# Three edits of order in a four-layer kernel: layer 0's theta and phi earlier in its loop, layer 1's first values between its scores, layer 2's first normalisation at the end of layer 1

## The reference

```python
# layer 0: attention between x and ctx over channels, then a batch norm over all batches
theta = Wtheta @ x + btheta;  phi = Wphi @ ctx + bphi;  g = Wg @ x + bg
y = softmax(phi.T @ theta) @ g.T
w = Wz @ y.T + bz
x = batchnorm(w) + x
# layer 1: latents (x) attend to [ctx, latents], 16 heads; then RMS norm and an MLP 512 -> 2048 -> 512
a = attention(q(latents), k(h), v(h), mask) @ out_w + out_b + latents
x = gelu(rmsnorm(a) @ w1 + b1) @ w2 + b2 + latents
# layer 2: a recurrent block
xa = layernorm(x);  sx = shifted(xa) - xa
t = tanh((xa + sx * maa_x) @ maa_w1)          # five mixes of 32
xm = xa + sx * (maa_stack + t @ maa_w2)       # inputs of k, w, v, r, g
...                                           # decayed sums over tokens, group norm, gate, feed forward
# layer 3: grouped attention on ctx, residual, layer norm
```

## Time and profile before

| | |
|---|---|
| time, median of 3 runs | 2301.31 us (2297.07 to 2303.19) |
| the profiled execution: its time, its span | 2297.31 us, 2295.5 us |
| TensorE, matmuls: busy, share | 2164.2 us, 94% |
| TensorE, weight loads (beside matmuls) | 1575.0 us, 69% |
| VectorE; ScalarE; POOL busy | 1132.5 us, 49%; 1164.1 us, 51%; 567.4 us, 25% |
| mean granted TensorE clock, share of full | 0.971 |
| layer 0; layer 1; layers 2 and 3 | 0 to 194 us; 194 to 1105.6; 1105.6 to 2295.5 |

### The profile page before, as it was taken

One profiled execution on the slowest core, in us unless ns is written; L12 is line 12 of the kernel. 1 busy time (PEld: TensorE's weight loads), 2 busy tenths in 40 slices (PEclk: granted clock), 3 DMA queues, 4 the chain that ended last, 5 costly groups with the idle time before them and its releaser, 6 DMA issues.

```text
span 2295.5 us, 56418 instructions
## 1 busy us (share of the span) xinstructions
PE 2164.2 (94%) x22208; PEld 1575.0 (69%) x22208; DVE 1132.5 (49%) x3132; ACT 1164.1 (51%) x3500; POOL 567.4 (25%) x573
## 2 busy tenths in 40 slices
PE   7886899999999999998579999999999999999986
PEld 3443666677777766776467778777777777777754
DVE  5664334333333333332345566655566655566643
ACT  4553444444444444553223566565566555556644
POOL 0001000011000100100344344443334444334420
PEclk9998899999999999999779999999999999999988
DMA  5531433443333333334401110101110001110100
GB/s 173 175 120 51 119 98 105 106 104 106 93 93 93 93 93 93 94 82 151 134 16 22 22 22 22 26 17 27 22 26 22 23 17 27 22 27 18 21 16 10
DMA packets 188381, 149.11 MB, mean 65 GB/s; under 512 B 85280, under 2 KB 163488, under 8 KB 185888
## 3 DMA queue, kind: packets, MB, share of 16 engines
q1 hardware_dynamic: 177920, 115.49, 19.8%
q10 hardware_dynamic: 8032, 18.35, 2.3%
q0 software_dynamic: 2240, 12.58, 1.6%
HBM read 96.04 MB, written 46.14 MB: 62 GB/s over the span
## 4 chain that ended last, share of the span: by engine, by line
PE 48%; ACT 1%; DVE 1%; issue 1%; POOL 0%; POOLq 0%; DVEq 0%; ACTq 0%
PE bank L1574 13%; PE bank L1580 12%; PE bank L1567 4%; PE quad L1702 4%; PE quad L1707 2%; PE quad L1821 2%; PE bank L1837 1%; PE quad L1698 1%; PE bank L1603 1%; PE quad L1623 1%; PE bank L1725 1%; PE quad L1712 1%; PE bank L1737 1%; PE bank L1642 1%; PE bank L1650 1%
## 5 line engine op out<-in xcount | busy, mean ns | idle before, releaser
L770 PEld LDWEIGHTS bank<-normedT,mlp_w 128*128 128x128 f32 x2048 | 232.6, 193 | 11.0 <-issue 10.0
L770 PE MATMUL bank<-normedT,mlp_w 128*128 128x128 f32 x2048 | 238.5, 278 | 0.8 <-DVE normedT L1020 0.8
L780 PE MATMUL bank<-mlp_w,geluT 128*128 128x512 f32 x512 | 224.7, 592 | 0.0
L2018 ACT ACTIVATE scores<-scores,nmax 128x128 f32<-128x128 f32 x512 | 198.3, 396 | 2.5 <-DVE nmax L2280 2.5
L1506 POOL TENSOR_TENSOR k_even_odd<-k_even_odd,decay_products 128x512 f32<-128x512 f32 x80 | 98.1, 1226 | 327.4 <-PE quad L1702 251.5
L780 PEld LDWEIGHTS bank<-mlp_w,geluT 128*128 128x128 f32 x512 | 95.0, 190 | 108.1 <-issue 108.1
L971 DVE CUSTOM_DVE_ANT_0 probs<-quad,neg_mask 128x256 f32<-128x256 f32 x256 | 90.8, 420 | 109.8 <-PE quad L725 109.8
L886 ACT ACTIVATE probs<-probs,nmax 128x256 f32<-128x256 f32 x256 | 126.6, 496 | 12.2 <-DVE nmax L971 11.8
L1434 POOL TENSOR_TENSOR gn_rstd<-gn_var_eps,halfs 128x32 f32<-128x32 f32 x16 | 87.0, 5435 | 170.1 <-DVE gn_var_eps L2203 170.1
L2168 DVE TENSOR_TENSOR rT<-rT,decay_products 128x256 f32<-128x256 f32 x96 | 40.9, 426 | 176.2 <-PE quad L1702 71.7
L2280 DVE CUSTOM_DVE_ANT_0 scores<-quad,mask 128x128 f32<-128x128 f32 x512 | 111.0, 286 | 31.9 <-PE quad L1821 31.9
(11 more groups left out here) (241 smaller groups left out, 4528.7 us busy)
## 6 DMA issues: line engine op xcount, KB each, us to landing
l_blocks<-probs_turned_blocks SPq DMA_DIRECT2D x128, 256.0 KB, 2.7
probsT<-l_blocks SPq DMA_DIRECT2D x256, 128.0 KB, 3.5
x_in<-in_x SPq DMA_DIRECT2D x32, 256.0 KB, 2.9
mlp_w<-in_mlp_w POOLq DMA_DIRECT2D x8, 1024.0 KB, 5.5
ctx_in<-in_ctx SPq DMA_DIRECT2D x16, 256.0 KB, 2.9
l_out<-wy ACTq DMA_DIRECT2D x16, 256.0 KB, 2.2
hT<-in_ctxT SPq DMA_DIRECT2D x16, 256.0 KB, 3.6
wy_in<-l_out SPq DMA_DIRECT2D x16, 256.0 KB, 4.0
```

The lines of the kernel that those rows point to most:

```text
L770: mm = nc.tensor.matmul(ps[:, f * P:(f + 1) * P], mlp_w1[:, c, m * P:(m + 1) * P], nT[:, c, :], start=(c == 0), stop=(c == NC - 1))
L780: mm = nc.tensor.matmul(PS[u.bank][:, :], gT[:, f, :], mlp_w2[:, f, :], start=(f == 0), stop=(f == NF - 1))
L2018: ac = nc.scalar.activation(s, s, ACT.Exp, bias=nmax[:, k, 2 * c + e:2 * c + e + 1], scale=-1.0, accum_out=rsum[:, kv, gr:gr + 1])
```

## The change

1. Layer 0, TensorE: `theta_phi(i + 1)` stands ahead of `out_y(i - 1)` and `scores(i, (2, 3))` instead of behind them. ScalarE: `copy_g(i)` comes ahead of `copy_y(i - 1)`, with a wait for `out_y` of its own (it overwrites the g that `out_y` reads), and `theta(i + 1)` waits until the second half of the scores has read the old theta.
2. Layer 1, TensorE: `values(0, 1)` between the two halves of batch 0's scores; ScalarE: `copy_latents(1)` before the second four groups of exponentials.
3. The norm of layer 2's batch 0 moves to the end of layer 1, on all engines, with the centring of Wv. The tiles of the norm are now made outside the layers, and four tiles of layer 1 share their memory (`wyin` with x, `xin1` with nx, `lat` with sx, `latb` with z). ScalarE no longer waits for the last store; SyncE does, before it issues the later stages' weights, which moves them from ScalarE's queue to SyncE's. Step 0 of the pipeline is now only `after_first`; waits for its zeros and constants go to the pieces that use them.

```diff
@@ layer0, tensor
                     turn_probs(i - 1, (2, 3))
+                    theta_phi(i + 1)
                     out_y(i - 1)
                     scores(i, (2, 3))
-                    theta_phi(i + 1)
                     g_proj(i + 1)
                     out_z(i - 1)
@@ layer0, scalar
                 def copy_g(i):
+                    if not isinstance(i, int) or i > 0:
+                        act.wait_ge(O.ready, O.written(i - 1, 1))
                     G.begin(i)
...
                     exp(i, 1)
+                    copy_g(i)
                     copy_y(i - 1)
-                    copy_g(i)
                     if not last:
+                        act.wait_ge(F.ready, F.written(i, 4))
                         theta(i + 1)
                         phi(i + 1)
@@ layer1, sync
                 move_probs(B - 1)
+                def load_x2(i):
+                    sp.dma_start(x2[:, :], l1_out[i]).then_inc(s_x, 16)
+                    sp.dma_start(row12[:, :], a["row1"][i]).then_inc(s_x, 16)
+
+                sp.wait_ge(s_lat, B)
+                sp.wait_ge(s_store, 48)
+                load_x2(0)
                 sp.wait_ge(O.free, O.read(B - 1, 2))
                 for t, n in zip((q_w, k_w, v_w, out_w), ("Wk", "Wr", "Wv", "Wg")):
                     sp.dma_start(t[:, :, :], a[n]).then_inc(s_w2, 16)
+                sp.wait_ge(s_nx1, 1)
+                sp.wait_ge(s_first1, 1)
+                load_x2(1)
@@ layer1, gpsimd
                 rms(B - 1)
+                pool.wait_ge(s_var1, 1)
+                nc.gpsimd.tensor_tensor(rstd2[:, :], ve2[:, :], halfs[:, 0:1], ALU.pow).then_inc(s_rstd1, 1)
+                pool.wait_ge(s_x, 32)
+                nc.gpsimd.tensor_copy(xaT2[:, :, 0], row12[:, :]).then_inc(s_first1, 1)
@@ layer1, tensor
                 scores(0, 0)
+                values(0, 1)
                 scores(0, 1)
-                values(0, 1)
                 turn_latents(1)
...
                 for j in range(4):
                     hidden(B - 1, j)
+                pe.wait_ge(s_nx1, 1)
+                pe.wait_ge(SR.free, SR.read(B - 1, NG))
+                for c in range(NC):
+                    mm = nc.tensor.transpose(PS[0][:, c * P:(c + 1) * P], nx2[:, c * P:(c + 1) * P], ident[:, :])
+                mm.then_inc(s_turn2, 1)
                 for j in range(4):
                     mlp_out(B - 1, j)
@@ layer1, scalar
                 copy_v(0, 1)
+                copy_latents(1)
                 for g in range(4, NG):
                     exps(0, g)
-                copy_latents(1)
...
                     gelu(B - 1, j)
+                act.wait_ge(s_turn2, 1)
+                for c in range(NC):
+                    ac = nc.scalar.activation(xaT2[:, c, 1:P + 1], PS[0][:, c * P:(c + 1) * P], ACT.Identity,
+                                              bias=C("ln1_b", c), scale=C("ln1_w", c))
+                ac.then_inc(s_xa2, 1)
                 store(B - 1)
-                act.wait_ge(s_store, 16 * (B + 1))
@@ layer1, vector
+                def first_norm():
+                    dve.wait_ge(s_x, 32)
+                    nc.vector.bn_stats(st62[:, :], x2[:, :]).then_inc(s_dveN, 1)
...
+                    dve.wait_ge(s_rstd1, 1)
+                    nc.vector.tensor_scalar(nx2[:, :], x2[:, :], mv2[:, 0:1], rstd2[:, :], ALU.subtract, ALU.mult).then_inc(s_nx1, 1)
...
+                    dve.wait_ge(s_w2, 16 * 4)
...
+                        nc.vector.tensor_tensor(wv, wv, wvm[:, c, :, :].unsqueeze(2).to_broadcast([P, NC, D2, HC]), ALU.subtract)\
+                            .then_inc(s_wv, 1)
+                    dve.wait_ge(s_latb2n, B)
+                    dve.wait_ge(s_xa2, 1)
+                    dve.wait_ge(s_first1, 1)
+                    nc.vector.tensor_tensor(sx2[:, :, :], xaT2[:, :, 0:P], xaT2[:, :, 1:P + 1], ALU.subtract).then_inc(s_dveN, 1)
...
                 copy_normed(B - 1)
+                first_norm()
                 output(B - 1)
@@ layers23, steps
-            for i in range(last):
+            segments["after_first"]()
+            for i in range(1, last):
                 step(*(i - k if i >= k else None for k in range(last + 1)))
-                if i == 0:
-                    segments["after_first"]()
@@ layers23, sync
-                load_x(0)
...
                 def after_first():
+                    n_lds0(0, None)
...
+                    sp.wait_ge(s_stored1, 16 * (B + 1))
                     for h in range(HC):
+                        sp.dma_start(W["Wo"][D2 * h:D2 * (h + 1), :, :], a["Wo"][h:P:HC, :, :]).then_inc(s_w3, 16)
+                    for n in ("Wfk", "Wfr", "Wfv"):
+                        sp.dma_start(W[n][:, :, :], a[n]).then_inc(s_w3, 16)
+                    for t, n in ((W["Wq3"], "Wq3"), (Wk3, "Wk3"), (Wv3, "Wv3")):
+                        sp.dma_start(t[:, :, :], a[n]).then_inc(s_w4, 16)
                     sp.wait_ge(s_wg, NC)
@@ layers23, scalar
-                for h in range(HC):
-                    act.dma_start(W["Wo"][D2 * h:D2 * (h + 1), :, :], a["Wo"][h:P:HC, :, :]).then_inc(s_w3, 16)
...
                 def after_first():
-                    act.wait_ge(s_zero, 4)
-                    act.wait_ge(s_setup, SETUP)
+                    pass
```

More of the change, by code:

```diff
@@ L459, in layer1 @@
 def layer1(nc, a, PS, sem, C, R, cols_of, ident, halfs, bn_scale, bn_shift, bn, inputs, load_x, load_ctx, loaded, l1_out,
-           weights, early, s_early, s_w2):
+           weights, early, s_early, s_w2, norm, norm_sems):
     stats, mv, bnt, s_bnv = bn
@@ L467, in layer1 @@
     q_w, k_w, v_w, out_w, mlp_w1, mlp_w2 = weights
+    x2, row12, st62, mv2, ve2, rstd2, nx2, xaT2, sx2, z2 = norm
+    s_x, s_var1, s_rstd1, s_nx1, s_first1, s_z, s_wvm, s_wv, s_dveN, s_stored1 = norm_sems
     NK = 2
@@ L1103, in turn, with layers23 @@
         self.n_ready = self.n_free = 0
-def layers23(nc, a, PS, quad, sem, C, R, CS, col_at, ident, hsum, halfs, l1_out, early, s_early, shared, s_w2):
+def layers23(nc, a, PS, quad, sem, C, R, CS, col_at, ident, hsum, halfs, l1_out, early, s_early, shared, s_w2,
+             norm, norm_sems):
+    x, row1, st6, mv, ve, rstd, nx, xaT, sx, z = norm
+    s_x, s_var1, s_rstd1, s_nx1, s_first1, s_z, s_wvm, s_wv, s_dveN, s_stored1 = norm_sems
     NU = 8
@@ L1907, in p_u1 @@
                 def p_u1(i, uses):
+                    if isinstance(i, int) and i == 0:
+                        act.wait_ge(s_zero, 4)
                     u, ps = use(uses, "p_u1")
@@ L1920, in p_k @@
                 def p_k(i, uses):
+                    if isinstance(i, int) and i == 0:
+                        act.wait_ge(s_setup, SETUP)
                     u, ps = use(uses, "p_k")
@@ L2375, in program @@
         s_w2 = sem("layer2_projections_loaded")
+        x = sb("x_in2", [P, D])
+        row1 = sb("state_row1", [P, NC])
+        st6 = sb("ln1_stats", [P, 6])
+        mv = sb("ln1_mean_var", [P, 2])
+        ve = sb("ln1_var_eps", [P, 1])
+        rstd = sb("ln1_rstd", [P, 1])
+        nx = sb("ln1_x", [P, D])
+        xaT = sb("xaT", [P, NC, P + 1])
+        sx = sb("shifted", [P, NC, P])
+        z = sb("z", [P, NC, P])
+        s_x = sem("n_x_loaded")
+        s_var1 = sem("n_ln1_var_ready")
+        s_rstd1 = sem("n_ln1_rstd_ready")
+        s_nx1 = sem("n_ln1_ready")
+        s_first1 = sem("n_first_row1_ready")
+        s_z = sem("n_z_ready")
+        s_wvm = sem("p_value_weight_sums_ready")
+        s_wv = sem("p_value_weights_centred")
+        s_dveN = sem("n_dve_step")
+        s_stored1 = sem("l1_x_stored")
+        norm = (x, row1, st6, mv, ve, rstd, nx, xaT, sx, z)
+        norm_sems = (s_x, s_var1, s_rstd1, s_nx1, s_first1, s_z, s_wvm, s_wv, s_dveN, s_stored1)
         w1_scope = ctx.enter_context(ExitStack())
```

83 lines of the change are left out of this document (35 added, 48 removed).

## The result

| | before | after |
|---|---|---|
| time, median (4 runs each) | 2299.20 us (2297.07 to 2303.19) | 2270.56 us (2267.56 to 2271.81) |
| profiled execution: time, span | 2297.31, 2295.5 us | 2269.75, 2267.9 us |
| TensorE matmuls busy | 2164.2 us, 94% | 2163.0 us, 95% |

The ratio is 0.9872, with an interval of 0.9852 to 0.9891: the kernel is 1.3% faster. TensorE does the same work. In the profiled pair the span is 27.6 us shorter, 26.4 of them TensorE's waiting, where 35.1 were forecast.

What follows compares the result with a forecast made beforehand. The kernel's time was taken as TensorE's work plus its waits, so only edits that remove or add a wait count. -14 - 2.2 - 18.9 = -35.1 us, from a median of 2301.3 to 2266; range 2256 to 2279.

Steps and rivals of the forecast that it cites:

- Part 1: Layer 0's loop: `theta_phi` ahead of `out_y` cuts the turn from 10.93 to 9.92 us, -14 us over 14 turns.
- S+3.0: Layer 0's turn, counted from S, the start of `out_y`: `scores(2, 3)` end and ScalarE's `theta` starts 3.0 us later.
- The inputs: Layer 0: next inputs land at S+7.4, `theta_phi` needs them at S+8.1, cover 0.7 us; longest landing stalls 0.1.
- rival E: Layer 0's input becomes the loop; at a 7 us landing the turn is 13.3 us and the kernel slower, 2314; chance 0.03.
- Rival B: Layer 0 gives only 9 us, since inputs or copies are later: 2271; chance 0.15.
- Part 2: Layer 1's start: values fill TensorE's wait before the second scores and the store-to-move chain shortens, -2.2 us.
- that chain gains once more: Layer 1's start, SyncE: first store to first move took 3.87 us against 2.57 unhindered; most of these 1.3 us goes.
- Part 3: Layer 1 to layer 2: moving the norm gives -17.4 us, the way to the first projection -1.5; -18.9 in all.
- rival D: Block change: VectorE sits in the centring, waiting for Wv, with `output` behind it, so nothing is won there; chance 0.04.
- rival C: Layer 2's start gives only 12 to 15 us, as POOL's reordering or another early step replaces the norm; chance 0.15.
- The clock at layer 2's start: First mixed product to first projection: -2.1 us if TensorE keeps its clock, 0 if it drops; -1.5 taken.
- Rival A: Layer 0: copies of chunks 0 and 1 don't hold TensorE, so it gives 17.6 us: 2263; chance 0.12.

Runs made afterwards that it cites:

- p1_only: The kernel before with the edits of layer 0 alone: 2291.01 us, ratio 0.9955.
- ctx_late: The changed kernel, with layer 0's input loads asked for one product later in the turn, from the fourth turn on: 2278.70 us, one run.
- no2b: The changed kernel, with ScalarE's `copy_latents(1)` put back behind the remaining exponentials: 2267.72 us, one run.
- x_late: The changed kernel, with SyncE asking for layer 2's first x only when VectorE has read the output product, 12 us later: 2271.25 us, one run.
- gate_again: The changed kernel with VectorE's copies of turned chunks 0 and 1 ahead of its fourth normalisation, timed in the changed kernel's second rounds: 2270.80 us, ratio 0.9871.
- after_again: The changed kernel itself, unaltered, run a second time: 2270.78 us, ratio 0.9871.
- storewait: The changed kernel, with ScalarE waiting again at the end of layer 1 for the last store of x: 2271.45 us, one run.
- actq: The changed kernel, with the 14 later weight loads issued by ScalarE at the start of layer 2 again: 2275.22 us, one run.
- gate: The changed kernel, with VectorE's copies of turned chunks 0 and 1 ahead of its fourth normalisation, first timing: 2267.71 us, ratio 0.9857.

## Why the prediction was right, and where it was off

The forecast was 2266, the measured median 2270.6 (2270.8 in the second set), inside the range of 2256 to 2279; faster, as expected at 0.95. The miss is 4.6 us. By the steps of the sum:

- **Part 1, forecast -14, measured -10.3 in the profiled pair (-10.4 by p1_only's ratio).** The mechanism was right, down to the wait that replaces the removed one: L255 for VectorE's copy, 0.27 where 0.25 was worked out, and L268 waiting in no turn of the loop. Two terms were mis-sized. First, the turn is 10.10, not 9.92: ScalarE's `theta` started 0.15 after the end of the scores rather than at it (S+3.15 for S+3.0), TensorE took up each chunk's turning some 0.14 us after VectorE's copy had ended, and `theta_phi` stood at S+8.29 for S+8.1. I had taken an end in the trace for the moment at which the next engine starts; 0.1 us at each of two handoffs, over 14 turns, is 2.5 us. (3.0 + 0.6 + 1.25 is 4.85, not the 4.87 of the sum; that changes nothing here.) Second, the first turn, where `theta_phi` waited 1.28 us for its input. I had worked out the cover of the inputs for a turn in the middle of the loop only. There `theta_phi` comes 5.36 us after `g_proj`; in the first turn, which has no `out_z` and no wait at L255, it would come after 3.96, from 18.64 to 22.60, and the input asked for at 20.23 landed 3.5 us later. 2.5 and 1.3 are the 3.8 missing. In the nine kernels with part 1 that were slow at the start the wait is 0.4 to 0.8 us (p1_only: 0.62, with a landing of 2.9), in the two others 1.28 and 1.34.
- **The inputs.** Issue at S+4.62 against the worked out S+4.52, landings 2.8, 2.9 and 3.5 (minimum, median, maximum), cover 0.7 forecast and 0.5 to 0.6 by ctx_late. In the loop the inputs bound no turn, so rival E is out for this kernel, though its loop is near: with one more product in front of the request it had begun. Rival B can't be called out. Layer 0's 10.3 is nearer its 9 than the forecast's 14, the total of 2270.6 is its 2271, and a part of its mechanism happened: the copies came 0.11 later than worked out, and the inputs were late in the first turn.
- **Part 2, forecast -2.2, measured -0.6 in the pair and -0.6 over the profiles.** The scores came earlier much as forecast (VectorE's second maxima 0.5 us, first store 0.7 where 0.9 was worked out). The step that failed is "that chain gains once more": I added a gain of 1.3 us on one link without following the chain to its end. In the pair the store-to-move distance fell by only 0.52, from 3.87 to 3.35, and from the moves' issue to their use it took more, 0.12 for the first half (7.54 for 7.42) and 0.45 for the second (238.31 - 229.96 = 8.35 for 249.26 - 241.36 = 7.90). In no2b the distance fell by 1.23, to 2.64, and the first half's landing took 1.25 of it back. Both come to 0.6. The statements that the second half of the attention would start 16 us earlier and the first projection of layer 2 35 us earlier were wrong: it was 10.95 and 27.39.
- **Part 3, forecast -18.9, measured -17.0 in the pair, and -19.5 to -19.8 where the clock stayed** (57.17, 57.11 and 56.88 us in x_late, gate_again and after_again, against 76.70). Step by step: the four transposes cost 0.43 (0.5 forecast); the first product of layer 2 is 1.68 us behind the output, where 1.8 was forecast; from it to the projection 9.25 us, where 9.5 was the full-clock end and I took 10.1 out of caution. VectorE's cover was 9.7 us (10 forecast), and the last of SyncE's moved issues went out at 1112.6, before batch 2's load at 1123.8. The centring waited for its weights (6.23 us) as rival D had it, but far inside its cover. ScalarE's 16 copies decide when the projection starts, but for 0.1 us: the short product behind them ends at 1106.34, POOL's addition at 1106.23, and the projection starts at 1106.37, 0.84 us after the short product's start, where it is 0.74 in no2b and storewait, in which POOL was done about 1 us or more before. So rival C's gain of only 12 to 15 is out, but POOL was as close as the 9.2 us had it: its addition ended 9.1 after the first product's start.
- **The clock at layer 2's start.** The row before had the granted clock at 0.50 there and a mix of 2.09 us. After, the mix took 1.17 in the profiled execution and in seven others, and 2.09 in no2b, actq and storewait. TensorE did not keep its clock over the stretch, though: it lost it behind the mix, while it waited 4.35 us for ScalarE's copies, where that cost next to nothing before the projection. The granted clock is the number before the last two (after, then no2b):

```profile
1102.00:1103.00 1.00, 0.00 (x0) 0.00 (x0) 0.81 (x4) 1.00 (x5) 1.00 (x2) 1.00 0.03 1
1103.00:1104.00 1.00, 0.00 (x0) 0.00 (x0) 1.00 (x1) 1.00 (x5) 1.00 (x2) 0.64 0.04 1
1104.00:1105.00 1.00, 0.00 (x0) 0.00 (x0) 0.97 (x3) 1.00 (x5) 1.00 (x1) 0.50 0.04 1
```
```profile
1097.00:1098.00 1.00, 0.41 (x2) 0.20 (x2) 0.97 (x7) 0.37 (x3) 1.00 (x2) 0.85 0.03 1
1098.00:1099.00 1.00, 0.70 (x12) 0.70 (x16) 0.88 (x6) 0.25 (x1) 1.00 (x4) 0.50 0.04 1
```

The rule in the Trainium skill (TensorE: Matmul & The Clock Gate, Part 1: The HAM clock gate), that the array falls back when it doesn't see sustained work, gave 0 instead of -1.5. The trace agrees that the clock falls in this stretch, and gives -2.4 for the change, because it falls late. It falls ahead of the mix where the gap before is 1.7 us longer (storewait), and once with the gap unchanged: in no2b, from output to projection 11.78 instead of 10.95.
- Rival A had layer 0 give 17.6 with the copies out of the way. They do hold TensorE, and taking that hold away (gate) brought a turn of 9.95, not 9.67, since the last normalisation and TensorE's own 0.15 come next.

The median moved 30.5 us from the 2301.3 that the prediction started from (2270.8), the profiled pair 27.6. Both executions of the pair started early, and before's lies 4.0 under its median for that; after's lost 2.9 again at the end of layer 1 and lies only 1.0 under. By the numbers above the account of the medians closes: 3.8 too much in part 1, 1.6 too much in part 2, 0.6 to 0.9 too little in part 3, 4.5 to 4.8 in all against 4.6. That it closes so well is in part luck, since it takes part 3 from the three executions with the most of it. Over all eight profiles that have part 3 unaltered or with x later the distance is 58.3 us on the mean, against 77.0 in the three without, -18.7 where -18.9 was forecast; with that, and 0.7 for the usual wait of the first turn, the account is 3.2, 1.6 and 0.2, 5.0 in all.

## What to carry to other kernels

When a removed wait is replaced by the next one, work the chain from start to start with the handoffs that the trace shows between engines, and check the first and last turn of the loop by themselves: here 0.1 us a handoff and the first turn made 3.8 of the 4.6 us of error. A gain on one link of a chain of transfers is no gain until the last link has been followed. Before a few microseconds are explained, run the same kernel twice: the 2.9 us of gate, and the 2.9 us at the end of layer 1, had a reason each until the second run took both away.

## What the runs showed of the hardware

- TensorE's clock makes much of the scatter of this kernel. At the start it kept its clock behind a wait of 1.59 us, or lost it there (granted 0.50 from 15.6 to 22.4 us in p1_only), or was slow up to 21 to 24 us from the first product on, 2.5 to 4.2 us apart at the first looped turn of the kernels with part 1; the product at the end of layer 1 took 5.1 to 6.6; and from the first projection of layer 2 to the end it took 1160.4 to 1164.6 us, with the same products in the same order. The Trainium skill (TensorE: Matmul & The Clock Gate, Part 1: The HAM clock gate) calls the warm-up variable from run to run; the traces agree, and show more than a warm-up: the clock was lost again in some executions, and kept in others of the same instructions, behind waits of 1.59 us at the start and of 1.72 to 1.75 us at layer 2's start.
- A wait of one engine at the end of a layer is one of all engines: 1.7 us of waiting for a store cost 1.7 on TensorE and another 1.5 through the clock.
- VectorE's normalisation of x took 3.41 us before, at the start of layer 2, and 0.55 in its new place, for the same 128x512. Before, it ran while POOL was zeroing tiles (1113.14 to 1116.2). The Trainium skill (SBUF — State Buffer, Who interferes with whom) says that VectorE's copies and scalings can take a pair of ports that is shared with GpSimd, where whoever issues first has it for the whole instruction and the other is blocked. The trace agrees that they hold each other up, but not on the order: VectorE's record starts at 1113.10, 0.04 us before the first of POOL's four zeroings, and ends at 1116.51, behind the last. The small constants of layer 2 now stand beside that zeroing instead, and one of them takes 1.59 us where it took 0.23, up to the end of the zeroing that began before it (1099.12 and 1099.10), but nobody waits for it.
